# The last mixture of experts of a vision tower: every expert on every token, or sorted rows in blocks of 256

## The chip, the cores and the metric

The kernel runs on one core of a Trainium2 chip, as one program. The metric is the time of one execution on the device in microseconds (us). Engines are named as the profile names them: PE is TensorE's matmul, PEld its weight load, DVE VectorE, ACT ScalarE, POOL GpSimd, and SP the sync engine, which here only issues DMAs.

## The reference

128 images become 65 tokens each (64 patches and a class token), so 8320 tokens of 128 numbers. Two attention layers and two mixtures of experts follow, each behind a layer norm and added to the running sum. Only the last mixture is touched by the change:

```python
def _L1_ffn_ref(x, gate_w, gate_b, w1, b1, w2, b2):   # E, K = 8 experts, 2 of them per token; H = 128
    logits = jnp.einsum('bsh,he->bse', x, gate_w) + gate_b
    topk_vals, topk_idx = jax.lax.top_k(logits, K)
    topk_weights = jax.nn.softmax(topk_vals, axis=-1)
    mask = jax.nn.one_hot(topk_idx, E, dtype=topk_weights.dtype)
    weights = jnp.einsum('bske,bsk->bse', mask, topk_weights)
    h = jax.nn.relu(jnp.einsum('bsh,ehf->bsef', x, w1) + b1)          # f = 256
    expert_out = jnp.einsum('bsef,efh->bseh', h, w2) + b2
    return jnp.einsum('bseh,bse->bsh', expert_out, weights)
...
    h = h + _L1_ffn_ref(_layernorm(h, axis=-1), ...)
```

The weights of six of the eight experts are zero for each token. All arithmetic here is float32.

## The kernel before

The program is a chain of stages, each a block of its own with barriers between them: patch embedding, layer norm, attention, layer norm, the first mixture (`routed_mlp`), layer norm, attention, layer norm, and the last mixture, `dense_mixture`. `h` (the running sum) and `xn` (its layer norm) stay in SBUF all the time as 128 partitions by 8320 tokens.

`dense_mixture` goes over 65 tiles of 128 tokens in a loop with two buffers (`pipelined`, two tiles written out per turn). For a tile POOL copies its columns of `xn` and `h`. PE computes the logits (L1370). DVE finds the two best and makes the weights (L1450 to L1471), with an exponential on ACT (L1414). PE applies all eight experts: `up` gives 16 products of 128x128x128 into two PSUM banks (L1348), which ACT reads with bias and relu into `hidden_m` (L1405). `down` gives 16 more (L1360). PE also turns the weights (L1377), adds the old sum and the second bias through two matmuls (L1385, L1387), which ACT copies into `acc_m` (L1428). DVE then adds expert by expert, each times its weight (L1484, eight instructions per tile), and SP stores the tile (L1320). PE's order in one turn is: logits and `up` of this tile, mixed with weights, `down` and base of the tile before.

Waits are on counting semaphores: `hid_ps` and `hid_sb` between PE and ACT, `acc_done` between DVE and PE.

## Time and profile before

| what | value |
|---|---|
| median of 3 runs | 2122.07 us (2121.67 to 2122.54) |
| the profiled execution's own time | 2128.26 us |
| its span, first to last instruction | 2126.5 us |
| PE busy over the span | 1999.7 us, 94% |
| DVE, ACT, POOL busy | 1147.3, 1035.9, 629.5 us |
| last mixture, in the trace | from 1578.6 us to the end |

Durations come from the profiled execution, which took 6.2 us longer than the median. Busy times of PE are those of pipelined instructions, so they say that the engine had work, not that it ran at its peak. A float32 product of 128x128x128 stands in the trace as two matmul records and two weight loads. DMA-issuing instructions do not count as busy on any engine.

### The profile page before, as it was taken

To read this page: it belongs to the slowest core of one execution; us is meant where nothing else is said; L and a number is where in the kernel's file an instruction comes from. 1 tells how busy PE (TensorE), PEld (TensorE's weight loads), DVE (VectorE), ACT (ScalarE), POOL (GpSimd) and SP (SyncE) were. 2 spreads that over 40 slices of the span, in tenths; PEclk is the share of its full clock that TensorE was granted. 3 is DMA by queue.
4 is the path that set the end of the run, shared out by engine and by line. 5 is a ranking of instruction groups with operands and counts; after the bars stand their busy time and mean duration, and the time that the engine had idled before them with its cause. 6 is when DMAs were issued, how large, how long until landed. Compare 5 with 4: busy or idle time off the path is not lost. (4 is left out here: it accounts for less than half of the span.)

```text
span 2126.5 us, 69078 instructions
## 1 busy us (share of the span) xinstructions
PE 1999.7 (94%) x27049; PEld 1538.0 (72%) x27049; DVE 1147.3 (54%) x3517; ACT 1035.9 (49%) x3106; POOL 629.5 (30%) x866
## 2 busy tenths in 40 slices
PE   8999978999999898799989999999889999999999
PEld 3444446766776666387747888888659999999999
DVE  0000057877777777466654555555455555555555
ACT  0000055655655554444455555555366555565555
POOL 0000007777777777001102433333300000000000
PEclk9999989999999999869999999999889999999999
DMA  9878400000000000200000000000000000000000
GB/s 380 309 302 319 191 1 3 4 3 3 3 3 3 3 3 3 89 1 1 1 1 2 3 2 2 2 2 2 2 1 10 7 7 9 7 9 7 7 9 9
DMA packets 30122, 91.84 MB, mean 43 GB/s; under 512 B 5972, under 2 KB 15324, under 8 KB 29660
## 3 DMA queue, kind: packets, MB, share of 16 engines
q1 hardware_dynamic: 28238, 87.25, 10.8%
q8 instruction: 180, 2.95, 0.6%
q10 hardware_dynamic: 1678, 1.43, 0.2%
q14 instruction: 26, 0.21, 0.0%
HBM read 84.41 MB, written 4.26 MB: 42 GB/s over the span
## 5 line engine op out<-in xcount | busy, mean ns | idle before, releaser
L1405 ACT ACTIVATE hidden_m<-ps,s_f_b 128x128 f32<-128x128 f32 x1040 | 296.3, 368 | 224.3 <-PE ps L1348 220.8
L830 PE MATMUL ps<-xn,s_a_wqkv 128*128 128x260 f32 x1024 | 289.2, 406 | 13.5 <-ACT qk_a L576 8.3
L1348 PE MATMUL ps<-xn,s_f_w 128*128 (+1 forms) x2080 | 287.5, 282 | 0.4 <-ACT hidden_m L1405 0.4
L1484 DVE SCALAR_TENSOR_TENSOR acc_m<-ps,weights_m,acc_m 128x128 f32<-128x128 f32 x520 | 182.4, 351 | 153.9 <-ACT acc_m L1428 105.0
L1348 PEld LDWEIGHTS ps<-xn,s_f_w 128*128 128x128 f32 x2080 | 255.1, 193 | 8.4 <-ACT hidden_m L1405 0.7
L168 PE MATMUL ps<-x_chunk,s_w_tok 128*128 128x512 f32 x576 | 251.9, 599 | 6.3 <-DMA x_chunk<-in_x_main 6.3
L1360 PE MATMUL ps<-s_f_w,hidden_m 128*128 128x128 f32 x2080 | 253.6, 275 | 0.0
L1360 PEld LDWEIGHTS ps<-s_f_w,hidden_m 128*128 128x128 f32 x2080 | 242.6, 192 | 1.6
L830 PEld LDWEIGHTS ps<-xn,s_a_wqkv 128*128 128x128 f32 x1024 | 176.3, 192 | 57.0 <-ACT qk_a L576 20.4
L168 PEld LDWEIGHTS ps<-x_chunk,s_w_tok 128*128 128x128 f32 x576 | 109.8, 192 | 147.1 <-issue 147.1
L1334 POOL COPY xn_tile_m<-xn 128x128 f32 (+1 forms) x65 | 19.1, 293 | 535.3 <-PE ps L1387 494.2
L649 ACT ACTIVATE e_a<-e_a 128x585 f32<-128x585 f32 (+1 forms) x128 | 85.2, 665 | 182.2 <-DVE e_a L741 93.7
L588 ACT ACTIVATE resT_a<-ps 128x260 f32<-128x260 f32 x256 | 84.6, 383 | 147.8 <-PE ps L847 120.6
L195 DVE SCALAR_TENSOR_TENSOR h<-ps,s_b_tok,s_pos 128x512 f32 (+1 forms) x16 | 11.3, 747 | 249.1 <-PE ps L176 249.1
L912 PE MATMUL ps<-s_a_wqkv,xn_pair_a 128*64 128x256 f32 x1024 | 139.0, 391 | 2.4 <-issue 1.0
L729 DVE TENSOR_REDUCE neg_max_a<-ps 128x8 f32<-128x520 f32 x128 | 89.4, 699 | 93.8 <-PE ps L808 93.7
L548 POOL TENSOR_TENSOR prob_a<-e_a,inv_sum_a 128x512 f32<-128x512 f32 x64 | 66.7, 1042 | 247.0 <-DVE inv_sum_a L772 179.8
L1510 ACT ACT_TABLE_LOAD x1 | 1.3, 1283 | 268.1 <-PEq L101 268.1
L870 PE MATMUL ps<-horner_a,probT_a 64*64 64x64 f32 x2048 | 109.2, 219 | 7.5 <-issue 7.3
L880 PE MATMUL ps<-probT_a,horner_a 64*64 64x65 f32 x2048 | 108.8, 223 | 1.5 <-DVE horner_a L688 1.5
L870 PE MATMUL ps<-dv_a,probT_a 64*64 64x64 f32 x2048 | 105.7, 218 | 4.5 <-ACT dv_a L625 3.1
L532 POOL TENSOR_TENSOR kept_a<-e_a,keep_a 128x585 f32<-128x585 f32 x64 | 87.2, 1362 | 75.9 <-issue 63.6
(197 smaller groups left out, 4074.2 us busy)
## 6 DMA issues: line engine op xcount, KB each, us to landing
x_chunk<-in_x_main SPq DMA_DIRECT2D x96, 768.0 KB, 8.5
out<-acc_m SPq DMA_DIRECT2D x65, 64.0 KB, 1.5
s_f_w<-in_f_w SPq DMA_DIRECT2D x2, 1024.0 KB
x_ends<-in_x_tail SPq DMA_DIRECT2D x16, 96.0 KB, 10.7
s_w_tok<-in_w_tok SPq DMA_DIRECT2D x6, 192.0 KB, 7.5
s_a_wqkv<-in_a_wqkv ACTq DMA_DIRECT2D x1, 768.0 KB
s_a_wqkv<-in_a_wqkv SPq DMA_DIRECT2D x1, 768.0 KB
s_f_w<-in_f_w SPq DMA_DIRECT2D x2, 256.0 KB
```

The costliest lines, as they stand in the source:

```text
L168: last = nc.tensor.matmul(ps[:, bank, :], w_tok[:, k, :], xb[:, s, k, :], start=(k == 0), stop=False)
L532: nc.gpsimd.tensor_tensor(columns(kept, t.even), columns(e_of(t), t.even), columns(keep, t.even), ALU.mult).then_inc(kept_done, 1)
L649: nc.scalar.activation(columns(e_of(t), t.even), columns(e_of(t), t.even), ACT.Exp, scale=-SCALE)\
L729: last = nc.vector.tensor_reduce(neg_max[:, :, 0:CH], score(), AX.X, ALU.min)
L830: nc.tensor.matmul(ps[:, QK_BANK[i], 0:QUAD], w_qkv[:, c * P:(c + 1) * P], xn[:, t.h * QUAD:(t.h + 1) * QUAD], start=True, stop=True).then ...
L870: last = nc.tensor.matmul(ps[rows, 2 + n, col:col + DH], pt[rows, k, c, i, 1:SEQ], values[rows, i, c, :], start=True, stop=True)
L880: last = nc.tensor.matmul(ps[other, R_BANK[i], c * SEQ:c * SEQ + cols], values[rows, (t.j - 6) % 2, i, c, :], pt[rows, k, c, i, 0:cols], s ...
L912: last = nc.tensor.matmul(ps[b * DH:(b + 1) * DH, V_BANK, i * CH * DH:(i + 1) * CH * DH] .rearrange("p (c d) -> p c d", c=CH), xs[:, k, i ...
L1348: last = nc.tensor.matmul(ps[:, b % 2, i * P:i * P + n], w1[:, c * P:(c + 1) * P], xn[:, bass.ds(a.index * n, n)], start=True, stop=True)
L1360: last = nc.tensor.matmul(ps[0:n, 2 + b, (e % 4) * D:(e % 4 + 1) * D], hid[:, a.slot, c, :], w2[:, c, :], start=(f == 0), stop=(f == F1 // ...
L1405: last = nc.scalar.activation(hid[:, a.slot, c, :], ps[:, b % 2, i * P:i * P + n], ACT.Relu, bias=b1[:, c:c + 1])
L1484: nc.vector.scalar_tensor_tensor(out=acc[0:n, sl, :], in0=ps[0:n, 2 + e // 4, (e % 4) * D:(e % 4 + 1) * D], scalar=wt[0:n, sl, e:e + 1], i ...
```

## The change

`dense_mixture` is replaced by `sparse_mixture`, which applies only the two chosen experts. It has three parts.

**Routing and sorting.** Tokens are taken in 5 groups of 13 tiles; a tile is every 65th token, so partition p of tile t is token 65p + t (`tile_of`). For a group PE makes logits, turns `xn` into rows of tokens, and counts with `before` and `all_ones` how many earlier tokens chose each expert (`ranks`). DVE turns that into a row number per token and choice. POOL then writes, for each tile and each of the two choices, 128 rows of 130 numbers (the token's vector, its name and its weight) to those rows of a buffer in memory, `regions[k]`, with one indirect DMA: 130 in all. The region of an expert holds 34 x 256 rows. SP writes filler rows behind each expert's last row. PE and ACT also make `base` (old sum and bias), which now stays in SBUF. A table of blocks (row and expert of each) is worked out on DVE.

**Blocks.** For each choice there are 40 blocks of 256 rows, so 80, whether they hold tokens or only filler. For a block SP reads its row number from the table and loads 256 rows. PE turns them (2 products), DVE copies the result out. PE does `up` (2 products of 256 columns), ACT one relu and DVE the other, PE does `down` (4 products), and DVE multiplies by each row's weight. ACT copies the weights of the block's expert, 514 columns, into one of four buffers, after reading the column from the table. POOL writes the result with two indirect DMAs of 128 rows to `acc[k]` in memory, at the tokens' own rows: 160 in all. These blocks are written out, not looped, with four buffers, `up` one block behind `turn_block`, and `down` two behind. The buffer of rows is free again when the copy `own` is done.

**Sum.** `acc[0]` is loaded into `xn`'s place during the second choice, on SP's queue between two block loads; `acc[1]` is loaded into `h`'s place after the last scatter has landed. Each is 13 DMAs. DVE adds both to `base`, 13 + 13 instructions, and SP stores 13 pieces.

Outside of the stage only the loading of this mixture's weights differs, into one tensor `f1_all` per expert.

```diff
+ROW = D + 2
+BLOCK_ROWS = 256
 
...
+def sparse_mixture(nc, tokens, h, xn, ps, ident, before, all_ones, gate_w, gate_b, expert_ids, w_all, b2,
+                   regions, acc, out):
...
+            for k in range(K):
+                def step(j, at, k=k):
+                    a = at(0)
+                    if a:
+                        g = a.index + k * NB
+                        row = sp.value_load(entry(row_i, k, a.index), min_val=0,
+                                            max_val=REGION * E1 + BLOCK_ROWS * (E1 - 1))
+                        freed(sp, own_done, g, R)
+                        sp.dma_start(blk[:, a.slot], regions[k][bass.ds(row, BLOCK_ROWS), :]
+                                     .rearrange("(h p) c -> p h c", p=P)).then_inc(loaded[a.slot], 16)
+                        if k == 1 and isinstance(a.index, int) and a.index == 2 * R - 1:
+                            for i in range(R):
+                                sp.wait_ge(added[i], 32 * NB // R)
+                            for c in range(PIECES):
+                                sp.dma_start(over_tiles(xn, c), in_memory(acc[0], c)).then_inc(piece_in[c], 16)
+                straight(sp, NB, R, 0, 2 * R, step)
+            for i in range(R):
+                sp.wait_ge(added[i], K * 32 * NB // R)
+            for c in range(PIECES):
+                sp.dma_start(over_tiles(h, c), in_memory(acc[1], c)).then_inc(last_in[c], 16)
+            for c in range(PIECES):
+                sp.wait_ge(finished, c + 1)
+                sp.dma_start(in_memory(out, c), base[:, c * PT:(c + 1) * PT, :]).then_inc(stored, 16)
+            sp.wait_ge(stored, 16 * PIECES)
...
+            for g in range(G):
+                pool.wait_ge(slot_done, g + 1)
+                for s, (t0, t1) in enumerate(SUBS):
+                    pool.wait_ge(xt_sb, S * g + s + 1)
+                    for t in range(t0, t1):
+                        for k in range(K):
+                            nc.gpsimd.indirect_dma_start(
+                                regions[k][:, :],
+                                bass.IndirectOffsetOnAxis(ap=slot_i[:, g % 2, t, k:k + 1], axis=0),
+                                rows[:, g % 2, t, 2 * k:2 * k + ROW], None).then_inc(sent[g % 2], 16)
+            for g in range(K * NB):
+                for half in range(2):
+                    pool.wait_ge(y_done, 2 * g + half + 1)
+                    nc.gpsimd.indirect_dma_start(
+                        acc[g // NB][:, :], bass.IndirectOffsetOnAxis(ap=goal[:, g % R, half:half + 1], axis=0),
+                        ys[:, g % R, half, :], None).then_inc(added[g % R], 16)
...
+            def logits(g):
+                for t in range(T):
+                    last = nc.tensor.matmul(logits_ps()[:, t, :], tile_of(xn, g * T + t), gate_w[:, :],
+                                            start=True, stop=True)
+                last.then_inc(l_ps, 1)
+
+                                                   tile_of(xn, g * T + t), ident[:, :])
+                    last.then_inc(xt_ps, 1)
...
+                nc.tensor.matmul(rank_at(), before[:, :], chosen[:, g % 2], start=True, stop=False)
+                for i in range(T):
+                    last = nc.tensor.matmul(rank_at()[:, i + 1:T + 1], all_ones[:, :],
+                                            chosen[:, g % 2, i:i + 1].to_broadcast([P, T - i, K, E1]),
+                                            start=False, stop=(i == T - 1))
...
+            logits(0)
+            turn_x(0)
+            ranks(0)
+            for g in range(G):
+                if g + 1 < G:
+                    logits(g + 1)
+                    turn_x(g + 1)
+                    ranks(g + 1)
+                turn_weights(g, 0)
+                for s in range(S):
+                    if s + 1 < S:
+                        turn_weights(g, s + 1)
+                    bases(g, s)
...
+            def turn_block(g, slot, k):
+                filled(pe, loaded[slot], g, slot, 16)
+                freed(pe, bt_sb, g, 2)
+                for half in range(2):
+                    last = nc.tensor.transpose(turned(slot)[:, half * P:(half + 1) * P], blk[:, slot, half, X_AT[k]],
+                                               ident[:, :])
...
+                for f in range(2):
+                    nc.tensor.matmul(ps[:, 1 + 2 * (slot % 2) + f, 0:BLOCK_ROWS], wb[:, slot, f * P:(f + 1) * P],
+                                     xt[:, slot % 2, :], start=True, stop=True).then_inc(up_ps, 1)
...
+                for half in range(2):
+                    for f in range(2):
+                        last = nc.tensor.matmul(ps[:, 5 + slot % 2, half * D:(half + 1) * D],
+                                                hid[:, slot % 2, f, half * P:(half + 1) * P],
+                                                wb[:, slot, F1 + f * P:F1 + (f + 1) * P],
+                                                start=(f == 0), stop=(f == 1))
...
+                    a = at(1)
+                    if a:
+                        up(a.index + k * NB, a.slot)
+                    a = at(0)
+                    if a:
+                        turn_block(a.index + k * NB, a.slot, k)
+                    a = at(2)
+                    if a:
+                        down(a.index + k * NB, a.slot)
...
+            def fetch_weights(g, slot, column):
+                freed(act, y_ps, g, R)
+                nc.scalar.activation(wb[:, slot, :], w_all[:, :, :].rearrange("p e c -> p (e c)")[
+                    :, bass.ds(column, WB)], ACT.Copy).then_inc(w_sb, 1)
...
+                    a = at(2)
+                    if a:
+                        act.wait_ge(w_sb, a.index + k * NB + 1)
+                        relu(a.index + k * NB, a.slot)
+                    a = at(0)
+                    if a:
+                        column = act.value_load(entry(col_i, k, a.index), min_val=0, max_val=WB * (E1 - 1))
+                        fetch_weights(a.index + k * NB, a.slot, column)
+                straight(act, NB, R, 2, R, step)
...
+            for g in range(G):
+                choose(g)
+                seat(g)
...
+            def copy_xt(g, slot, k):
+                dve.wait_ge(bt_ps, g + 1)
+                freed(dve, up_ps, g, 2, 2)
+                nc.vector.tensor_copy(xt[:, slot % 2, :], ps[:, 7 * (slot % 2), 0:BLOCK_ROWS]).then_inc(bt_sb, 1)
+                freed(dve, y_done, g, R, 2)
+                nc.vector.tensor_copy(own[:, slot], blk[:, slot, :, OWN_AT[k]]).then_inc(own_done, 1)
...
+            def relu(g, slot):
+                dve.wait_ge(up_ps, g * 2 + 2)
+                freed(dve, y_ps, g, 2)
+                nc.vector.tensor_scalar(hid[:, slot % 2, 1, :], ps[:, 2 + 2 * (slot % 2), 0:BLOCK_ROWS],
+                                        wb[:, slot, 2 * F1 + 1:2 * F1 + 2], 0.0, ALU.add, ALU.max).then_inc(hid1, 1)
...
+            def weigh(g, slot, k):
+                dve.wait_ge(own_done, g + 1)
+                emptied(dve, added[slot], g, slot, 32)
+                nc.vector.tensor_copy(goal[:, slot], own[:, slot, :, NAME[k]])
+                dve.wait_ge(y_ps, g + 1)
+                for half in range(2):
+                    nc.vector.tensor_scalar(ys[:, slot, half, :], ps[:, 5 + slot % 2, half * D:(half + 1) * D],
+                                            own[:, slot, half, WEIGHT[k]:WEIGHT[k] + 1], None,
+                                            ALU.mult).then_inc(y_done, 1)
...
+            for c in range(PIECES):
+                dve.wait_ge(piece_in[c], 16)
+                nc.vector.tensor_tensor(base[:, c * PT:(c + 1) * PT, :], base[:, c * PT:(c + 1) * PT, :],
+                                        over_tiles(xn, c), ALU.add).then_inc(summed, 1)
+            for c in range(PIECES):
+                dve.wait_ge(summed, c + 1)
+                dve.wait_ge(last_in[c], 16)
+                nc.vector.tensor_tensor(base[:, c * PT:(c + 1) * PT, :], base[:, c * PT:(c + 1) * PT, :],
+                                        over_tiles(h, c), ALU.add).then_inc(finished, 1)
...
-        dense_mixture(nc, tokens, h, xn, ps, S["ident"], S["f1_gate"], S["f1_gate_b"], S["expert_ids"],
-                      S["f1_w1"], S["f1_b1"], S["f1_w2"], S["f1_b2"], out)
+        sparse_mixture(nc, tokens, h, xn, ps, S["ident"], S["before"], S["all_ones"], S["f1_gate"], S["f1_gate_b"],
+                       S["expert_ids"], S["f1_all"], S["f1_b2"], regions, acc, out)
```

The next rows are PE's instructions, in the middle of the last mixture, before: one tile's turn of the loop (`s_f_w` in L1348 is the first weight, in L1360 the second; register instructions stand between).

```order
L1370 MATMUL ps<-s_f_gate,xn_tile_m 128x8
L1348 MATMUL ps<-xn,s_f_w 128x128 x4
L1377 MATMUL ps<-s_ident,weights_m 8x128
L1360 MATMUL ps<-s_f_w,hidden_m 128x128 x8
L1348 MATMUL ps<-xn,s_f_w 128x128 x4
L1385 MATMUL ps<-s_ident,h_tile_m 128x128
L1387 MATMUL ps<-s_f_b,weightsT_m 128x128
```

After these come 4, 8 and 4 more of L1348, L1360 and L1348. In the changed kernel the same place on PE, one step of the blocks (line numbers are the changed kernel's: L1545 turns rows, L1555 is `up`, L1564 is `down`):

```order
L1555 MATMUL ps<-pad_rows_m,rows_m 128x256 x2
L1545 MATMUL ps<-s_ident,rows_m 128x128 x2
L1564 MATMUL ps<-rows_m,pad_rows_m 128x128 x4
```

So 37 products a tile, 65 times, become 8 products a block, 80 times, and `up` now has 256 columns. On POOL, the end of its program was two copies a tile:

```order
L1334 COPY xn_tile_m<-xn 128x128
L1335 COPY h_tile_m<-h 128x128
```

Now POOL's part of the stage reads (L1463 the scatters into `regions`, L1470 those into `acc`):

```order
L1452 MEMSET pad_rows_m 128x4224
L1455 IOTA pad_rows_m 128x32 x2
L1463 DMA expert_rows<-rows_m,slot_i_m 71680x130 x130
L1470 DMA out_rows<-pad_rows_m,block_goal_m 12416x128 x160
```

All 290 indirect DMAs stand in one row on POOL's one queue, and it does nothing else. On ACT one step of the blocks is this (L1652 reads the column, L1635 copies the weights, L1641 is the relu):

```order
L1652 TENSOR_LOAD block_column_m
L1652 ISA x2
L1635 ISA
L1635 ACTIVATE rows_m<-s_f_all 128x514
L1641 ACTIVATE pad_rows_m<-ps,rows_m 128x256
```

Where ACT had 16 relus of 128 columns a tile, it has now two instructions a block and a read into a register ahead of them.

## Rows read from the trace of the kernel before

**Rows 1.** The page: span, then busy time of each engine.
```profile
span 2126.5 us, 69078 instructions
PE 1999.7 (94%) x27049; PEld 1538.0 (72%) x27049; DVE 1147.3 (54%) x3517; ACT 1035.9 (49%) x3106; POOL 629.5 (30%) x866
```
**Rows 2.** Busy time by stretch: the mixture, inside it, and the patch embedding's loads.
```profile
core 0: us, PE busy (x) PEld busy (x) DVE busy (x) ACT busy (x) POOL busy (x), PEclk, DMA share, GB/s
1578.60:2126.50 547.90, 543.48 (x4615) 525.82 (x4615) 305.19 (x1365) 322.48 (x1236) 34.29 (x130) 0.99 0.03 8
1600.00:1700.00 100.00, 100.00 (x857) 96.83 (x856) 56.28 (x252) 59.42 (x229) 6.44 (x25) 1.00 0.03 8
60.00:160.00 100.00, 100.00 (x238) 43.29 (x237) 4.23 (x6) 0.00 (x0) 0.00 (x0) 1.00 0.82 318
```
**Rows 3.** Waits in the mixture: who waited for whom, us, times, longest.
```profile
POOL xn_tile_m L1334 <- PE ps L1387: 494.2, 63, 11.7
ACT hidden_m L1405 <- PE ps L1348: 220.8, 194, 8.5
```
**Rows 4.** The chain that ended last, mixture: shares, then one piece.
```profile
by line: PE ps L1348 45.7%; PE ps L1360 42.3%; PE ps L1387 4.9%; PE ps L1385 2.6%; PE ps L1370 1.5%; PE ps L1377 1.3%; ACT hidden_m L1405 0.4%; DVE acc_m L1484 0.3%; ACT L1414 0.2%; issue 0.1%; POOL xn_tile_m L1334 0.1%; POOL h_tile_m L1335
...
1612.73 1.79 PE ps L1360 x16
```
**Rows 5.** Groups by line, PE: busy us, mean ns of one.
```profile
L168 PE MATMUL ps<-x_chunk,s_w_tok 128*128 128x512 f32 x576 | 251.9, 599 | 6.3 <-DMA x_chunk<-in_x_main 6.3
L1370 PEld LDWEIGHTS ps<-s_f_gate,xn_tile_m 128*128 128x128 f32 x130 | 19.9, 194 | 2.6 <-POOL h_tile_m L1335 2.6
```
**Rows 6.** Groups by line, DVE and ACT.
```profile
L704 DVE COPY probT_a<-ps 128x512 f32<-128x512 f32 x64 | 44.3, 692 | 101.5 <-PE ps L945 101.5
L723 DVE TENSOR_TENSOR h<-ps,h 128x256 f32 x26 | 11.1, 425 | 0.0
L741 DVE TENSOR_SCALAR e_a<-ps,neg_max_a 128x65 f32<-128x65 f32 x64 | 17.7, 277 | 0.0
L1459 DVE CAST index_m<-index_m 128x2 f32<-128x2 uint32 x65 | 11.0, 169 | 2.3
L1454 DVE MAX8 top_m<-logit_m 128x8 f32<-128x8 f32 x65 | 10.7, 165 | 2.8
L613 ACT ACTIVATE v_raw_a<-ps 128x512 f32<-128x512 f32 x64 | 38.2, 597 | 29.1 <-PE ps L912 28.7 <-POOL v_alpha_a L536 0.4
L588 ACT ACTIVATE resT_a<-ps 128x260 f32<-128x260 f32 x256 | 84.6, 383 | 147.8 <-PE ps L847 120.6 <-PE ps L880 27.0
```
**Rows 7.** Groups by line, POOL.
```profile
L1334 POOL COPY xn_tile_m<-xn 128x128 f32 x60 | 17.6, 293 | 467.0 <-PE ps L1387 467.0
L548 POOL TENSOR_TENSOR prob_a<-e_a,inv_sum_a 128x512 f32<-128x512 f32 x64 | 66.7, 1042 | 247.0 <-DVE inv_sum_a L772 179.8 <-issue 67.1
L478 POOL MEMSET cls_queries_a<- 128x1040 f32 x2 | 1.9, 965 | 345.9 <-POOLq L219 345.9
```
**Rows 8.** The output tile's stores: issue in ns (min/median/max), and us to landing.
```profile
L1320 SPq DMA_DIRECT2D out<-acc_m x65: 332/332/353, 1595.6 to 2124.6; - x65
...
DMA to landing us min/median/max: 1.5/1.5/2.7
```
**Rows 9.** Windows between stages and in the first mixture.
```profile
1520.00:1530.00 10.00, 7.34 (x147) 5.89 (x151) 5.45 (x10) 3.44 (x11) 5.08 (x8) 1.00 0.01 2
1530.00:1550.00 20.00, 12.17 (x72) 8.13 (x69) 1.12 (x3) 6.16 (x11) 1.11 (x2) 0.57 0.00 1
900.00:940.00 40.00, 35.48 (x154) 32.13 (x155) 22.59 (x103) 14.88 (x32) 0.00 (x0) 0.50 0.00 1
```

More of the change, by code:

```diff
@@ L36 @@
 EPS = 1e-5
+REGION = 34 * 256
 BANK = 512
 CHUNK_IMAGES = 8
+ROW = D + 2
+BLOCK_ROWS = 256
 class At:
@@ new lines, in sparse_mixture @@
+        pad_i = sb("pad_place_m", [P, K, E1], I32)
+        base = sb("base_m", [P, TILES, D])
+        limit = sb("limits_m", [P, K, E1, LB])
+        over = sb("over_limit_m", [P, K, E1, LB])
+        blocks = sb("blocks_of_m", [P, K, E1])
+        upto = sb("not_after_m", [P, E1, E1])
+        part = sb("prefix_terms_m", [P, K, E1, E1])
+        end = sb("end_block_m", [P, K, E1])
+        number = sb("block_number_m", [P, NB])
+        past = sb("past_m", [P, K, NB, E1])
+        gone = sb("gone_m", [P, K, NB, E1])
@@ new lines, in _ @@
+            nc.gpsimd.iota(number[:, :], [[1, NB]], base=0, channel_multiplier=0,
+                           allow_small_or_imprecise_dtypes=True).then_inc(consts, 1)
+            nc.gpsimd.memset(pad[:, :, :, :], 0.0).then_inc(pads_made, 1)
+            pool.wait_ge(pads_made, 1)
+            for column in (1, D + 2):
+                nc.gpsimd.iota(pad[:, :, :, column], [[BLOCK_ROWS, 2 * E1], [P, 2]], base=tokens,
+                               channel_multiplier=1, allow_small_or_imprecise_dtypes=True).then_inc(pads_made, 1)
@@ L1488, in _, with chained, settle, ids @@
-            pipelined(dve, tokens // n, SL, D_, SL, step)
+            done = [0]
+            def chained(ins):
+                done[0] += 1
+                ins.then_inc(chain, 1)
+            def settle():
+                dve.wait_ge(chain, done[0])
+            def ids(shape, axes):
+                t = expert_ids[:, 0:E1]
+                for a in axes:
+                    t = t.unsqueeze(a)
+                return t.to_broadcast(shape)
+            nc.vector.memset(chosen[:, :, T], 0.0)
@@ new lines, in _ @@
+            settle()
+            for k in range(K):
+                last = nc.vector.tensor_tensor(part[:, k], blocks[:, k, :].unsqueeze(1).to_broadcast([P, E1, E1]),
+                                               upto[:, :, :], ALU.mult)
+            chained(last)
+            settle()
+            chained(nc.vector.tensor_reduce(end[:, :, :], part[:, :, :, :], AX.X, ALU.add))
+            settle()
+            for k in range(K):
+                last = nc.vector.tensor_tensor(past[:, k], number[:, :].unsqueeze(2).to_broadcast([P, NB, E1]),
+                                               end[:, k, :].unsqueeze(1).to_broadcast([P, NB, E1]), ALU.is_ge)
@@ new lines, in _ @@
+            chained(last)
+            settle()
+            for k in range(K):
+                last = nc.vector.tensor_tensor(gone[:, k], past[:, k], blocks[:, k, :].unsqueeze(1)
+                                               .to_broadcast([P, NB, E1]), ALU.mult)
+            chained(last)
+            chained(nc.vector.tensor_reduce(expert[:, :, :], past[:, :, :, :], AX.X, ALU.add))
+            settle()
+            chained(nc.vector.tensor_reduce(first[:, :, :], gone[:, :, :, :], AX.X, ALU.add))
@@ new lines, in _ @@
+            settle()
+            chained(nc.vector.tensor_scalar(base_row[:, :, :], expert[:, :, :], float(REGION), None, ALU.mult))
+            for k in range(K):
+                last = nc.vector.tensor_tensor(row_f[:, k, :], number[:, :], first[:, k, :], ALU.subtract)
+            chained(last)
+            settle()
+            chained(nc.vector.scalar_tensor_tensor(out=first[:, :, :], in0=row_f[:, :, :], scalar=float(BLOCK_ROWS),
+                                                   in1=base_row[:, :, :], op0=ALU.mult, op1=ALU.add))
@@ L1605, in vit_tower @@
         h = ctx.enter_context(nc.sbuf_tensor("h", [P, tokens], FP32))
+        assert tokens + BLOCK_ROWS <= REGION and REGION % BLOCK_ROWS == 0
+        regions = [nc.dram_tensor(f"expert_rows{k}", (E1 * REGION + E1 * BLOCK_ROWS, ROW), FP32, kind="Internal").ap()
+                   for k in range(2)]
+        acc = [nc.dram_tensor(f"out_rows{k}", (tokens + 2 * E1 * BLOCK_ROWS, D), FP32, kind="Internal").ap()
+               for k in range(2)]
         xn = ctx.enter_context(nc.sbuf_tensor("xn", [P, tokens], FP32))
```

495 lines of the change are left out of this document (304 added, 191 removed).

## The prediction

> **What bounds the kernel now.** I read the busy times first. PE is at 94% of the span, no other engine above 54% [rows 1]. A share over the whole span says little about one stage, so I cut the trace: the last mixture runs from 1578.60 us to the end, 547.9 us, and PE is busy for 543.5 of them, at a granted clock of 0.99 [rows 2]. The waits agree: POOL and ACT wait for PE (494 and 221 us) and no long wait of PE for anyone stands there [rows 3]. The chain that ended last is PE for 98% of this stretch [rows 4]. So the stage is worth what its matmuls cost.
>
> What one costs comes from the stretch of 100 us in which PE never stops: 857 matmul records [rows 2]. A tile has 71 records (65 tiles; 64 for `up` and `down`, 7 for the rest), so 857/71 = 12.07 tiles, 8.28 us each. A piece of the chain has 16 records of `down` in 1.79 us, 0.112 us a record, or 0.224 us for a float32 product of 128 columns [rows 4]. 64 records are 7.17 us of the 8.28. The other 1.11 us are four products (logits, turned weights, two for the base), 0.28 us each. With 512 columns a record takes 251.9/576 = 0.437 us [rows 5]; between the two, 256 columns take about 0.22 us a record, 0.44 us a product.
>
> The profiled execution took 2128.26 us, the median is 2122.07. I work out the stage's new length, and apply the difference to the median.
>
> **What the change takes away.** The whole stage, 547.9 us. What stands outside of it keeps its instructions, except for loads of weights that fall early and are hidden in both.
>
> **What it adds, part by part.** The unknown that decides is c, the time that one indirect DMA of 128 rows holds POOL's queue. There are 130 + 160 of them, in order, on one engine. No row of the trace shows one. From below, SP needs 0.332 us to issue a plain DMA of 128 rows [rows 8], where hardware makes the addresses. From above, if POOL were held until the data lands, it would be issue and landing, 0.33 + 1.5 = 1.83 us [rows 8]. In between, POOL's instruction on 512 elements takes 1.04 us, its copy of 128 columns 0.29 us [rows 7]. An indirect DMA makes an address for each of 128 rows in software, one by one, which is nearer to POOL's long instruction than to its copy. I take c = 1.3 us, between 1.04 and 1.83, and keep 0.33 and 1.83 as ends.
>
> The Trainium skill, DMA: Bandwidth & Descriptors, section on the anatomy of a DMA from GpSimd, gives about 2.0 us plus the bytes over 436e3 per DMA, mostly the receipt at its end. An estimate by that page, if the whole term held the queue for 64 KB, is 2.15 us; the sum below would then be 708 us instead of 461. The page itself puts most of it behind the issue, where it can overlap, and no row here tells which.
>
> 1. *Start, 16 us.* The first scatter needs logits, chosen experts, ranks and row numbers of group 0. PE: 13 logits and 13 turned tiles at 0.28 to 0.56 us (the upper end at half clock, since the granted clock was 0.57 between the last attention and its layer norm [rows 9]), some 9 us, then 14 small rank products, 2 us. DVE runs 26 instructions of the MAX8 kind, 0.165 us each or less when they follow one another [rows 6], and about ten more: 7 us, partly beside PE. Row numbers: five instructions of up to 208 elements, 2 us. POOL's memset of 4224 columns costs 4224/1040 x 0.965 = 3.9 us [rows 7] and is hidden in this.
>
> 2. *Scatters of tokens, 130 x 1.3 = 169 us.* Beside them PE has, per group of 13 tiles, 65 products at 0.28 and the ranks: 18.2 + 2 = 20 us, against 26 x 1.3 = 34 us on POOL. DVE has about 9 us, ACT less. They are hidden while c is over 0.78 us; without that cover the part costs 100 us. Another price that the trace does not show is the weight load from every 65th column: 39 products a group read so. A load of 128 neighbouring columns takes 0.19 us [rows 5]; if such a one took twice that, two to a product, PE's group grows by 39 x 2 x 0.19 = 15 to 35 us, level with POOL: still nothing. SBUF — State Buffer in the Trainium skill, its remark on cachelines, says that each access to a new 16-byte line pays a penalty, which speaks for that price; no row here reads so.
>
> 3. *Handover, 10 us.* The last scatter lands (1.5 us [rows 8]), SP reads a row number and loads 133 KB (2 to 3 us), and a first block goes through turn, copy, `up`, relu, `down` and the multiply, about 4 us, before POOL has work again. The table of blocks is made while POOL still scatters group 4.
>
> 4. *Blocks, 80 x 2.8 = 224 us.* POOL: 2 x 1.3 = 2.6 us a block. PE: two turns 0.45, `up` 2 x 0.44 = 0.88, `down` 4 x 0.224 = 0.90, so 2.23 us. DVE: two instructions of 256 columns at 0.425, two of 128 at about 0.3, two tiny ones at 0.17 [rows 6], 1.8 us. ACT: a copy of 514 columns 0.60 and a relu of 256 at 0.38 [rows 6], 0.98 us, and a register read that the trace does not show: between nothing and a landing, 1.5 us [rows 8], so at most 2.5 us. DMA: the output tile's 128 rows are a share of 0.03 of 16 engines [rows 2], 0.03 x 16 x 8.28/128 = 0.03 us a row; 512 rows a block over 16 engines are 1.0 us. POOL sets the pace with four engines close behind it, so I add 0.2 us for steps in which one of them is late.
>
> 5. *Loading the first sum, 6 us.* SP puts 13 DMAs, 4.26 MB, between two block loads on its queue. At 318 GB/s [rows 2] that is 13.4 us, and the next block load lands about 16 us later. Four buffers cover 4 x 2.8 = 11 us. The rest is a stall of the blocks, with the drain between the two choices about 6 us in all.
>
> 6. *End, 36 us.* After the last product POOL scatters twice, 2.6 us, and 1.5 us pass until they land. Then 4.26 MB come in and 4.26 MB go out, 8.52 MB/318 GB/s = 26.8 us, and two landings and the issue of the first piece, 4 us. DVE adds 26 pieces of 640 columns, at (692/512) x 640 = 0.86 us each [rows 6] 22 us, half before the loads are in. Sum 35, taken as 36.
>
> 16 + 169 + 10 + 224 + 6 + 36 = 461 us, against 547.9: 87 us less. The median would be 2122.07 - 87 = **2035 us**. As a function of c the stage is 84 + 290c, where 84 = 16 + 10 + 6 + 36 + 80 x 0.2; it equals 547.9 at c = 1.60 us. At c = 1.15 to 1.5 it is 417 to 519, the result 1991 to 2093.
>
> **The rivals.**
>
> *Cheap scatters.* If a scatter costs as POOL's 512-element instruction does, 1.04 us, the tokens take 135 us, and a block 2.5 us, paced by PE and ACT: 16 + 135 + 10 + 200 + 6 + 36 = 403, result 1977. For it: the work of an indirect DMA on POOL moves no data. Against: it makes two times 128 addresses. At c = 0.33 PE paces both parts: 16 + 100 + 10 + 184 + 6 + 36 = 352, result 1926.
>
> *Slower: a scatter holds POOL.* At c = 1.83, where it waits for its own landing, the stage is 84 + 531 = 615, result 2189. It decides from c = 1.60 on. For it: every row moves by its own address and one engine makes them all, and the changed program has nothing to put beside them but a wait. Against: on SP's queue the next issue does not wait for the landing before it.
>
> *The clock.* Where the work on PE gets thin its granted clock falls to half: 0.57 between the last attention and layer norm with 12 of 20 us busy, but also 0.50 in the first mixture with 35 of 40 us busy; with 7.3 of 10 us busy in the last attention it was 1.00 [rows 9]. Blocks that leave PE idle for 0.6 us in 2.8 may fall on either side. At 1.2 GHz a block costs PE 2 x 2.23 = 4.46 us, 357 instead of 224, and the groups 40 us instead of 34, 30 more in all: 461 + 133 + 30 = 624, result 2198. With only the blocks slow for half of the time it is 461 + 66 = 527, result 2101. Against the full fall: at half speed PE would be busy all the time, and in long stretches of full work it had its full clock.
>
> **How the numbers follow.** Chances: my forecast (c from 1.1 to 1.6) 0.50; cheap scatters 0.15; a scatter that holds POOL 0.23; the clock, or a chain between engines as slow as it, 0.12. The likeliest case alone reaches from 1991 to 2093. The range that holds 8 in 10 goes from 1950, below the cheap case, to 2185, nearly to the held one. What a measurement of this kernel can tell is about 0.2%, 4 us. Faster: 0.48 of the first, all of the second, a third of the last: 0.67. Within 0.2%: 0.03. Slower: 0.30.
>
> **What would show it.** In the changed profile: the scatters into `regions` follow each other at a steady distance, which is c, and the sum of the first part is 130 times that (step 2). Blocks: 2.8 us from one load of SP to the next, and DVE waiting for `added`, the landed scatters, more than for PE (step 4). If DVE instead waits for PE and PEclk reads 0.5, it is the clock. A gap of some 6 us in PE at the eighth block of the second choice is step 5. From the last block to the end about 36 us with high GB/s (step 6). The prediction is wrong if c is outside of 1.1 to 1.6, or if a step of the blocks is over 3.3 us while POOL is idle.

## The result and the profile after

The changed kernel takes **2000.96 us** (median of 4 runs, 1999.92 to 2006.15) against 2122.31 us of the kernel before, run beside it (2121.67 to 2124.63): a ratio of 0.9431, 95% interval 0.9413 to 0.9449, 121 us less. The forecast was 2035, with a range of 1950 to 2185. The profiled execution took 2000.72 us.

The page, span and busy times, against [rows 1]:

```profile
span 1998.7 us, 60392 instructions
PE 1753.3 (88%) x24144; PEld 1274.2 (64%) x24144; DVE 1020.6 (51%) x2949; ACT 835.0 (42%) x2096; POOL 881.3 (44%) x1033
```

POOL has gained 252 us of work and PE lost 246; a reader of this row alone would still call PE the bound. The stage shows otherwise. It now runs from 1571.10 us to the end, 427.6 us instead of 547.9, and the windows of busy time cut it as the prediction did, into start, scatters of tokens, handover, blocks and end; the last window is a steady piece of the blocks (compare [rows 2]):

```profile
1571.10:1584.70 13.60, 12.66 (x62) 11.82 (x62) 6.56 (x56) 3.33 (x6) 5.37 (x7) 0.50 0.61 126
1584.70:1749.40 164.70, 110.70 (x530) 97.90 (x529) 32.21 (x235) 28.52 (x60) 125.10 (x130) 0.58 0.22 68
1749.40:1762.70 13.30, 7.97 (x25) 6.14 (x26) 2.96 (x11) 3.48 (x6) 0.00 (x0) 0.50 0.30 75
1762.70:1972.50 209.80, 169.91 (x1097) 149.41 (x1095) 126.56 (x482) 85.05 (x154) 154.94 (x160) 0.93 0.40 118
1972.50:1998.70 26.20, 0.00 (x0) 0.00 (x0) 10.53 (x13) 0.00 (x0) 0.00 (x0) 0.50 0.88 328
...
1800.00:1850.00 50.00, 43.82 (x278) 37.79 (x278) 29.05 (x119) 21.23 (x39) 37.81 (x41) 1.00 0.37 105
```

In a steady 50 us of the blocks PE is busy for 43.8 us and POOL for only 37.8, and yet POOL is the bound. Its groups by line say why: behind "idle before" almost all of the time stands under "issue", that is, nobody kept it waiting.

```profile
L1470 POOL DMA_INDIRECT out_rows<-pad_rows_m,block_goal_m x160 | 154.9, 968 | 68.2 <-issue 43.3 <-DVE pad_rows_m L1800 24.9
L1463 POOL DMA_INDIRECT expert_rows<-rows_m,slot_i_m x130 | 125.1, 962 | 47.5 <-issue 39.3 <-DVE slot_i_m L1734 8.2
```

A scatter is 0.96 us busy and 0.30 us of gap that belongs to it: **c = 1.263 us** from start to start, the mean of the 91 scatters of the blocks between 1762.71 and 1877.67 us; in the first part it is 164.7/130 = 1.267. The waits between 1578 and 2000 us (who waited for whom, us, times, longest; compare [rows 3], where POOL waited 494 us for PE):

```profile
POOL out_rows L1470 <- issue: 43.3, 142, 0.3
DVE block_goal_m L1797 <- DMA out_rows<-pad_rows_m,block_goal_m: 56.1, 54, 2.0
POOL out_rows L1470 <- DVE pad_rows_m L1800: 24.9, 18, 13.6
```

DVE waits 54 times for a scatter's landing. POOL waits for DVE's products for 24.9 us in all, and 19.8 of these are two gaps: the handover (13.6, of which 0.3 belongs to c) and one gap of 6.2 us in the second choice, the stall of step 5 in the prediction (the timeline of POOL):

```profile
1877.67 0.96 POOL L1470 DMA_INDIRECT out_rows<-pad_rows_m,block_goal_m  x1 [0.30 <-issue]
1884.81 0.96 POOL L1470 DMA_INDIRECT out_rows<-pad_rows_m,block_goal_m  x1 [6.18 <-DVE pad_rows_m L1800]
1886.07 0.96 POOL L1470 DMA_INDIRECT out_rows<-pad_rows_m,block_goal_m  x1 [0.30 <-issue]
```

On SP's queue the cause stands ahead of it: the 13 loads of the first sum take 8.6 us to issue, 0.3 to 1.0 us each, and the block load behind them lands 8.3 us after its own issue instead of about 2 (first the SP timeline, then the chain that ended last):

```profile
1864.85 7.80 SPq L1431 DMA_DIRECT2D xn<-out_rows  x13
1873.41 21.64 SPq L1425 DMA_DIRECT2D rows_m<-expert_rows  x10
...
1873.41 8.29 DMA rows_m<-expert_rows
1881.75 0.69 PE ps L1545 x2
1882.44 1.71 PE ps L1564 x8
```

The load that comes late is the ninth of the second choice, but POOL's gap lies ahead of the seventh block's scatters. PE does its products in the program's order, and the program has the turn of a block ahead of the `down` of the block two before it. So PE stands at the ninth block's turn for 8.5 us, while the seventh block's `down`, which needs nothing of that load, waits behind it.

### The profile page after: what moved, and what is told of

Its sections match the earlier page's. It is cut to its first block and busy times, and to the rows that moved or that the text cites. A ratio compares the mean times of both kernels' runs of the same rounds, so it can differ in the third digit from the quotient of the medians.

```text
span 1998.7 us, 60392 instructions
## 1 busy us (share of the span) xinstructions
PE 1753.3 (88%) x24144; PEld 1274.2 (64%) x24144; DVE 1020.6 (51%) x2949; ACT 835.0 (42%) x2096; POOL 881.3 (44%) x1033
## 3 DMA queue, kind: packets, MB, share of 16 engines
q8 instruction: 191, 3.13, 0.6%
## 5 line engine op out<-in xcount | busy, mean ns | idle before, releaser
L1470 POOL DMA_INDIRECT out_rows<-pad_rows_m,block_goal_m x160 | 154.9, 968 | 68.2 <-issue 43.3
L1463 POOL DMA_INDIRECT expert_rows<-rows_m,slot_i_m x130 | 125.1, 962 | 47.5 <-issue 39.3
L1555 PE MATMUL ps<-pad_rows_m,rows_m 128*128 128x256 f32 x320 | 90.8, 408 | 18.1 <-issue 15.8
L1261 POOL TENSOR_TENSOR h<-h,mlp_gated 128x320 f32<-128x320 f32 x26 | 22.4, 863 | 187.9 <-DVE mlp_gated L1241 187.9
L579 ACT ACTIVATE qk_a<-ps 128x260 f32<-128x260 f32 x256 | 92.2, 388 | 28.6 <-PE ps L833 25.3
L883 PE MATMUL ps<-probT_a,cls_values_a 64*64 64x1 f32 x2048 | 91.8, 187 | 6.0 <-issue 5.7
```

What stands on the lines that cost most here:

```text
L579: nc.scalar.activation(qk[:, t.j // 2, c, :], ps[:, QK_BANK[i], 0:QUAD], ACT.Identity if bias is not None else ACT.Copy, bias=bias[:, i:i ...
L883: last = nc.tensor.matmul(ps[other, R_BANK[i], c * SEQ:c * SEQ + cols], values[rows, (t.j - 6) % 2, i, c, :], pt[rows, k, c, i, 0:cols], s ...
L1463: nc.gpsimd.indirect_dma_start(regions[k][:, :], bass.IndirectOffsetOnAxis(ap=slot_i[:, g % 2, t, k:k + 1], axis=0), rows[:, g % 2, t, 2 * ...
L1470: nc.gpsimd.indirect_dma_start(acc[g // NB][:, :], bass.IndirectOffsetOnAxis(ap=goal[:, g % R, half:half + 1], axis=0), ys[:, g % R, half, ...
L1555: nc.tensor.matmul(ps[:, 1 + 2 * (slot % 2) + f, 0:BLOCK_ROWS], wb[:, slot, f * P:(f + 1) * P], xt[:, slot % 2, :], start=True, stop=True) ...
```

## The experiments

Twelve runs. Apart from the totals I give the stage by itself, from its first logits product (1571.1 us in the changed kernel) to the end. That product starts anywhere between 1570.0 and 1576.3 us in these traces, although the code ahead of it is the same, so a total carries noise of up to 6 us that the stage doesn't.

| run | time, us (runs) | ratio to before, 95% interval | stage, us | against 427.6 |
|---|---|---|---|---|
| extra_128 | 2096.35 (2) | 0.9869 (0.9842 to 0.9897) | 523.3 | +95.7 |
| extra_64 | 2095.11 (2) | 0.9864 (0.9837 to 0.9891) | 517.7 | +90.1 |
| extra_thin | 2095.85 (2) | 0.9867 (0.9840 to 0.9894) | 523.0 | +95.4 |
| half_down | 2001.82 (4) | 0.9424 (0.9403 to 0.9445) | 427.0 | -0.6 |
| load_spread | 1994.95 (5) | 0.9395 (0.9383 to 0.9408) | 422.3 | -5.3 |
| blocks_early | 1993.30 (5) | 0.9385 (0.9372 to 0.9397) | 417.0 | -10.6 |
| early_spread | 1983.31 (5) | 0.9346 (0.9333 to 0.9359) | 407.8 | -19.8 |
| bases_first | 2004.99 (5) | 0.9445 (0.9430 to 0.9459) | 427.5 | -0.1 |
| extra_8 | 2216.34 (2) | 1.0430 (1.0399 to 1.0460) | disturbed | |
| extra_plain | 2111.90 (3) | 0.9938 (0.9916 to 0.9961) | disturbed | |
| down_twice | 2124.14 (8) | 0.9997 (0.9972 to 1.0021) | disturbed | |
| down_twice_again | 2031.89 (4) | 0.9566 (0.9550 to 0.9582) | 455.8 | +28.2 |

My theory: POOL's queue sets the pace at c for each indirect DMA, and all else is hidden up to 2 x c = 2.53 us a block. The first rival: PE, or a chain through it, sets the pace, since it is the busier engine.

**Does POOL pace, and what is c made of?** A third indirect DMA in each block:

```diff
+                nc.gpsimd.indirect_dma_start(
+                    scratch[:, :], bass.IndirectOffsetOnAxis(ap=goal[0:128, g % R, 0:1], axis=0),
+                    ys[0:128, g % R, 0, 0:128], None).then_inc(added[g % R], 16)
```

extra_64 has `goal[0:64 ...]` and `ys[0:64 ...]`, extra_thin `ys[..., 0:16]`. In all of them a block's buffers count as free only when the third DMA has landed too (48 instead of 32 on `added`).

> Every block of the second part gets a third indirect DMA on POOL, of 128 rows of 128 numbers into a tensor that nobody reads: 80 more in all, nothing is left out, and the block's buffers come free only when it has landed too. Theory (POOL's queue sets the pace of the blocks, 1.263 us for each indirect DMA): 80 x 1.263 = 101 us more than the changed kernel's 2001, less up to 6 us because four buffers then cover more of the stall at the first sum's load: 2096 to 2102, and the distance between scatters stays 1.26. Rival (PE or a chain of engines sets the pace and POOL has room of its own): less than 60 us more. A third case: with 3.8 us a block PE is busy for about half of the time only; if its granted clock falls to 0.5 a block costs PE 4.0 to 4.4 us, 2115 to 2150, and POOL shows idle time that PE ends.

> As extra_128, but the third indirect DMA of a block writes 64 rows of 128 numbers instead of 128 rows. It asks what the 1.26 us of a scatter are made of. If they are paid for each row (an address made for each in software, as I argued before the result), the extra one costs 0.63 us and the kernel takes 80 x 0.63 = 50 us more than 2001, 2051; its busy time on POOL reads 0.48 us. If they are paid for each instruction, it costs as much as extra_128, 2102. In between (0.3 us of issue and the rest by rows): 0.78 us each, 2063.

> As extra_128, but the third indirect DMA of a block writes 128 rows of only 16 numbers (64 bytes instead of 512). If POOL's 1.26 us are paid for making addresses or for each instruction, it costs as much as extra_128: 2096 to 2102. If they are paid for moving the bytes (the queue takes no more until the data has been drained), the extra one costs about an eighth of that and the issue, 0.3 to 0.45 us, and the kernel takes 2025 to 2037.

extra_128 came out as the theory of the pace said: 80 x 1.263 = 101.0, less 5.9 for the gap at the first sum's load (6.18 less the 0.30 of any scatter), which is gone, is 95.1; the stage grew by 95.7. The distance stayed 1.26. The other two settle what c is. The groups by line of extra_128, extra_64 and extra_thin, in this order:

```profile
L1474 POOL DMA_INDIRECT scratch_rows<-pad_rows_m,block_goal_m x80 | 77.4, 967 | 24.4 <-issue 24.4
```
```profile
L1474 POOL DMA_INDIRECT scratch_rows<-pad_rows_m,block_goal_m x80 | 72.6, 908 | 24.4 <-issue 24.4
```
```profile
L1474 POOL DMA_INDIRECT scratch_rows<-pad_rows_m,block_goal_m x80 | 77.4, 967 | 24.4 <-issue 24.4
```

An eighth of the bytes costs the same, and half of the rows saves 0.06 us of 0.96. So c is paid for each instruction, hardly for rows, not for bytes. The guess that c is made of rows gave 2051 us for extra_64, 44 us too little.

> As extra_64, but the third indirect DMA of a block writes only 8 rows. POOL's busy time was 0.96 us for 128 rows and 0.905 us for 64, a slope of 0.85 ns a row. If this line goes on, 8 rows take 0.86 us busy and 1.16 us with the issue, and the kernel takes 80 x 1.16 = 93 us more than the changed kernel's 2001, less the 6 to 7 us that the other extras showed: 2086 to 2089. If the price for few rows is a small one (a step per row or per 64 rows), it takes 2025 to 2045.

> As extra_128, but the third DMA of a block is a plain one on POOL's queue, 128 rows of 128 numbers to neighbouring rows of the unread tensor, with no indices. If the 1.26 us belong to any DMA that POOL's software prepares, it costs the same, 2094 to 2098. If they belong to the indirect form, the plain one holds POOL for about as long as SP's 0.33 us or less, and the kernel takes at most 80 x 0.4 = 32 us more than 2001: 2001 to 2033.

extra_plain's third DMA is `nc.gpsimd.dma_start(scratch[g * P:(g + 1) * P, :], ys[:, g % R, 0, :])`. Both totals missed: in these two and in down_twice engines stood still in the scatters of tokens (below). What the extra DMA costs can still be read where POOL has its work in time. The timeline of extra_8, then that of extra_plain:

```profile
1873.43 0.88 POOL L1474 DMA_INDIRECT scratch_rows<-pad_rows_m,block_goal_m  x1 [0.30 <-issue]
1874.62 1.00 POOL L1471 DMA_INDIRECT out_rows<-pad_rows_m,block_goal_m  x1 [0.30 <-issue]
```
```profile
1871.31 0.96 POOL L1471 DMA_INDIRECT out_rows<-pad_rows_m,block_goal_m  x1 [0.30 <-issue]
1872.28 0.58 POOL L1474 DMA_DIRECT2D scratch_rows<-pad_rows_m  x1
1873.15 0.98 POOL L1471 DMA_INDIRECT out_rows<-pad_rows_m,block_goal_m  x1 [0.30 <-issue]
```

Eight rows hold POOL for 0.88 us and the gap, 1.18 us, against 1.16 expected. A plain DMA holds it for 0.58 us and has no gap ahead of it; a block takes 3.13 us instead of 2.53, so it costs 0.60 us, half of an indirect one and nearly twice SP's 0.332 us [rows 8].

**Is PE hidden, and by how much?** half_down takes two of the four products of `down` away, so that its output lacks half of the second layer's sum; down_twice does all four twice, with the same output. Of half_down's edit (the first two lines; `start` and `stop` follow it) and down_twice's (the last two):

```diff
-                    for f in range(2):
+                    for f in range(1):
...
-                for half in range(2):
+                for half in (0, 1, 0, 1):
```

> PE leaves out the second half of the hidden layer in down: 2 products of 128 columns a block instead of 4, so the output holds half of the second layer's sum. Nothing else changes. Theory (POOL paces the blocks at 2.53 us, and PE, which does a step in 1.98 us when work is queued for it, waits): no change, 1998 to 2003. Rival (PE, or a chain through it, paces the blocks): 80 x 0.45 = 36 us less, 1965; one third of that, 1989, if PE paces only the blocks in which it runs slow or catches up. A fall of the granted clock with the thinner work would make it slower, by up to 80 x 0.6 = 50 us.

> PE does the 4 products of down twice in each block, 0.9 us more work at full clock; the output is the same. A step of PE that has its work queued took 1.98 us in the changed kernel, so it takes 2.88 us here, more than POOL's 2.53. Theory (PE is hidden up to 2.53 us and sets the pace above that): 80 x 0.35 = 28 us more than 2001, less what of the two stalls is caught up, 2025 to 2032, and POOL now waits for DVE's rows in most blocks. Rival (PE and POOL take turns instead of overlapping, so that each us on PE is a us on the blocks): 80 x 0.9 = 72 us more, 2073. If PE's own step were longer than I read (2.4 us), 62 us more.

> The same program as down_twice, run again, since in the three kernels that ran together (extra_8, extra_plain, down_twice) PE and ACT stood still for some 90 us in the scatters of tokens, whose code those kernels don't change. If that belongs to the chip or the moment of that call, the scatters of tokens now follow each other without a gap (164 us from first to last, not 240), and the kernel takes what the theory of PE's pace says: 2025 to 2032 if PE's step is 2.88 us, 2073 if every us of PE counts. If it belongs to the program (where its code lies), the gaps are there again at the same places and the time is 2115 to 2130.

half_down changed nothing (stage -0.6 us), though PE was then busy for 34.8 instead of 43.8 us in the window 1800 to 1850: 9 us less work in 50, not one of them on the path. The rival falls. down_twice_again took 28.2 us more, as expected from 80 x (2.88 - 2.53), and its waits from 1765 to 2020 us have turned round: POOL waits 78 times, DVE for PE instead of for landings.

```profile
POOL out_rows L1470 <- DVE pad_rows_m L1800: 71.7, 78, 14.8
DVE pad_rows_m L1800 <- PE ps L1564: 66.7, 80, 2.3
```

Its timeline of PE gives one step, 1833.94 to 1836.81, 2.87 us without a gap:

```profile
1833.94 1.03 PE L1555 MATMUL ps<-pad_rows_m,rows_m 128*128 128x256 f32 x4
1834.81 0.38 PE L1545 MATMUL ps<-s_ident,rows_m 128*128 128x128 f32 x2
1835.03 1.95 PE L1564 MATMUL ps<-rows_m,pad_rows_m 128*128 128x128 f32 x16
1836.81 1.03 PE L1555 MATMUL ps<-pad_rows_m,rows_m 128*128 128x256 f32 x4
```

Of these, 0.89 us are the second `down` (what one took in the changed kernel's chain at full clock). So PE needs 2.87 - 0.89 = 1.98 us a block in the changed kernel, and 0.55 us of slack lie in each 2.53.

The first run of this program took 2124 us, 92 more. What was different comes under "The stand-still".

**Can the two gaps be taken out?** load_spread puts one load of the first sum behind every second block load:

```diff
-                            for c in range(PIECES):
+                        if k == 1 and isinstance(a.index, int) and 2 * R - 1 <= a.index < 2 * R - 1 + 2 * PIECES \
+                                and (a.index - 2 * R + 1) % 2 == 0:
+                            c = (a.index - 2 * R + 1) // 2
```

blocks_early lets the first choice's blocks start while the second choice's last 13 scatters still run:

```diff
+                for ks in ((0, 1),) if g + 1 < G else ((0,), (1,)):
...
+                                    .then_inc(sent[g % 2] if g + 1 < G or k == 0 else late, 16)
...
+                if k:
+                    sp.wait_ge(late, 16 * T)
```

> The 13 loads of the first sum go to SP's queue one at a time, each behind every second block load, instead of all 13 ahead of one block load; nothing is left out. Theory: the block load that today queues behind 4.26 MB comes 8.5 us late for PE and leaves POOL idle for 6.2 us once; spread, no block load is later than 2 us and the four buffers cover that. 6 us less than the changed kernel's 2001: 1994 to 1997, and no gap of over 1 us in POOL's row of scatters in the second choice. Rival (the stall is paid back by blocks that follow faster, or each small load costs a little of its own): no change, 1999 to 2003.

> In the last group of tokens POOL writes the 13 tiles' rows of the first choice first, then the 13 of the second; SP loads the first choice's blocks as soon as the first choice's rows have landed and only the second choice's blocks wait for the rest. The rings of block rows and weights move to places that are free by then. Nothing is left out. Theory: the handover of 13.3 us, in which POOL has no work, comes to lie beside 13 x 1.263 = 16.4 us of scatters: about 12 to 13 us less, 1988 to 1990, with no gap of POOL over 1.5 us between the two rows of scatters. Rival (the filler rows, the table of blocks or the first PE steps at half clock are late too, so that the blocks can't start so early): a gain of 5 us or less, 1996 to 2001.

> The edits of load_spread and blocks_early together. Theory: two stalls in different places of one row of 290 scatters, so the gains add: 18 to 20 us less than the changed kernel's 2001, 1981 to 1983, and 6.5% less than the kernel before (ratio 0.934). If one gap only makes room for another (PE late after the earlier start, say), less than 14 us.

load_spread came out as expected: 5.3 us in the stage, and the gap is gone. blocks_early fell short: 10.6 us in the stage instead of 12 to 13, and a total of 1993.30 us instead of 1988 to 1990. The handover vanished, with 1.26 us from the last scatter of tokens to the first of a block (its timeline of POOL):

```profile
1753.47 0.96 POOL L1467 DMA_INDIRECT expert_rows<-rows_m,slot_i_m  x1 [0.31 <-issue]
1754.73 0.96 POOL L1475 DMA_INDIRECT out_rows<-pad_rows_m,block_goal_m  x1 [0.30 <-issue]
```

but the second gap grew from 6.2 to 7.3 us, and beside it stood two of 0.7 and 1.35 us. With both edits the gains more than add, 19.8 us in the stage against 18 to 20 expected (the second gap goes at its larger size), and POOL's waits in the stage of early_spread leave nothing to take away:

```profile
POOL out_rows L1477 <- issue: 40.2, 132, 0.3
POOL expert_rows L1469 <- issue: 39.3, 129, 0.3
POOL out_rows L1477 <- DVE pad_rows_m L1806: 8.5, 28, 0.3
```

No wait of POOL is over 0.3 us there but the first, for row numbers: from the first scatter to the end of the last it is 367.9 us, and 290 x 1.263 = 366.3. At 1983.31 us (ratio 0.9346) this version beats both kernels; it is faster than the changed one by 17.7 us in the totals, and the two intervals are apart.

**Does the order of ranks and base rows matter?** bases_first moves `logits(g + 1)`, `turn_x(g + 1)` and `ranks(g + 1)` on PE, and `exponential` and `copy_x` on ACT, behind the base rows of group g.

> Undoes one part of the change, the ranks ahead of base rows: PE and ACT do a group's base rows first and the logits, turned rows and ranks of the next group behind them. Nothing is left out. Theory: POOL's 26 scatters of a group take 33 us and PE's work for a group 20 to 28 us, so the order inside of a group is hidden: 2001, or up to 4 us more at the second group. Rival (the order matters: DVE's chain from ranks to row numbers then ends behind POOL's last scatter of the group before): 3 to 8 us more at each of four groups, 2013 to 2033, seen as POOL waiting for DVE's row numbers.

The stage is 427.5 us against 427.6, and POOL waits only once for row numbers, at the start, 8.2 us as before. So this part of the change is worth nothing here. The total is 4.0 us higher; in the profiled execution the stage starts 4.2 us later, and nothing was edited ahead of it.

**The stand-still.** extra_8, extra_plain and down_twice ran on the same chip. In all three the scatters of tokens, which none of them edits, took some 50 us longer, and POOL waited for row numbers of a later group three times, 28.0, 11.4 and 11.5 us; the handover was 27 to 29 us. In extra_8 and down_twice the later steps of the blocks were uneven as well; in extra_plain only one gap stood there, 2.7 us. ACT's timeline in down_twice, where the changed kernel has gaps of 2 to 3 us at these lines:

```profile
1596.24 1.13 ACT L1596 ACTIVATE rows_m<-ps 128x384 f32<-128x384 f32 x2 [0.63 <-issue]
1618.41 0.59 ACT L1605 ACTIVATE weightsT_m<-ps 8x512 f32<-8x512 f32 x1 [21.03 <-remote]
1625.42 0.48 ACT L1605 ACTIVATE weightsT_m<-ps 8x384 f32<-8x384 f32 x1 [6.42 <-remote]
1661.81 0.60 ACT L1613 ACTIVATE base_m<-ps 128x512 f32<-128x512 f32 x1 [35.91 <-remote]
```

"remote" is a wait for which the trace has no releaser. The same program on another chip had none of this and took 2031.89 us, so the program alone doesn't bring it about; whether the chip or the moment did can't be told. extra_8 and extra_64, one number apart, say the same. The kernel before ran beside them at its usual 2123.47 us. PE was fully at work again only when POOL had run out of scatters at about 1654 us: busy for 19.2 us of 1670 to 1690, after 0.7 of 1630 to 1650. One guess is that code was fetched late while POOL's DMAs ran, since this stage is written out straight. The trace's DMA records of the instruction queues don't bear it out. In down_twice_again packets of 16 KB start at 1591.7, 1609.2 and 1638.9 us; in down_twice one starts at 1591.0 and the next only at 1665.8, but ACT and PE are at work again at 1661.8 and 1662.5, ahead of it. The missing packets may be a consequence of the stand-still as well as its cause, and the cause stays open.

## Why the prediction was right

The decision was right for its reason: one queue, 290 indirect DMAs in a row, at c = 1.263 us against 1.3 assumed and a break-even of 1.60. The size was less good: the stage was 33 us shorter than the sum, so the change saved 121 us where 87 were forecast. The five windows above against the sum:

| step | forecast | measured | off by |
|---|---|---|---|
| 1 start | 16 | 13.6 | -2.4 |
| 2 scatters of tokens | 169 | 164.7 | -4.3 |
| 3 handover | 10 | 13.3 | +3.3 |
| 4, 5 blocks and first sum's load | 224 + 6 | 209.8 | -20.2 |
| 6 end | 36 | 26.2 | -9.8 |
| sum | 461 | 427.6 | -33.4 |

- *Step 1.* PE was busy for 12.7 of 13.6 us at a granted clock of 0.50, as the dearer price assumed.
- *Step 2.* Hidden as forecast: PE was busy for 110.7 of 164.7 us at a granted clock of 0.58. The load of every 65th column is settled by the weight loads' groups by line. First from 1596 to 1598 us (granted clock 1.00), where L1516 reads every 65th column and L1520 neighbours, then from 1753 to 1762 us (0.50), where L1555 reads neighbours:

```profile
L1516 PEld LDWEIGHTS ps<-s_ident,h 128*128 128x128 f32 x7 | 1.7, 327 | 0.0
L1520 PEld LDWEIGHTS ps<-s_f_b,weightsT_m 8*128 8x128 f32 x4 | 0.5, 185 | 0.1
```
```profile
L1555 PEld LDWEIGHTS ps<-pad_rows_m,rows_m 128*128 128x128 f32 x10 | 2.9, 325 | 2.3 <-issue 1.0 <-ACT rows_m L1635 1.0
```

L1520 loads only 8 rows, but the blocks' loads of neighbours with 128 rows take as long, 0.189 us for L1555 from 1800 to 1850 us at 1.00. So at full clock the stride makes it 0.327 us instead of 0.19, 1.7 times as much and not 2; at half clock a load of neighbours takes 0.325 us as well, and L1516 took 0.325 us on average over the whole of this part, so there the stride costs nothing. The Trainium skill, SBUF — State Buffer, remark on cachelines, says that an access to a new 16-byte line pays a penalty; the trace agrees at full clock and shows no such penalty at half clock.
- *Step 3, short by 3.3.* The first steps of PE ran at half clock, and its program puts three blocks' turns and two `up` ahead of the first `down`. The chain that ended last (start, us, what):

```profile
1754.79 2.04 PE ps L1555 x4
1756.83 0.44 PE ps L1545 x2
...
1757.87 2.04 PE ps L1555 x4
...
1760.34 1.71 PE ps L1564 x8
```

`up` took 2.04 us where later blocks take 0.87. From the first turn, at 1753.52, to the end of that `down` it was 8.5 us, and I had about 4 for all of this.
- *Step 4, mis-sized.* "I add 0.2 us for steps in which one of them is late" was the largest error, 16 us. Almost no step was late: 75 of the 79 distances from block to block were 2.52 to 2.54 us, and the other four were the gap, the block behind it and the last two. The second is 0.037 x 160 = 6 us in c. PE's own price was too high as well, 2.23 against 1.98, because I priced a turn as two records and it has one (0.22 us for both halves); nothing hung on it. The rows had the count: a tile's seven other records are two each for logits and the two base products, and one for the turned weights. With 16 + 16 for `up` and `down` that also makes 36 products a tile, not 37.
- *Step 5.* 6.18 us against 6, and load_spread shows the cause by taking it away. The late load landed 16.9 us after the first of the 13 was issued, against about 16. The drain between the two choices, which the 6 us also held, made no gap on POOL. That the gap's size was met is in part luck, since the sum went by the four buffers alone and not by the `down` that stood behind the late turn on PE.
- *Step 6, over by 9.8.* 2.6 us were counted twice, since the last two scatters are part of the 80 blocks. 1 us was rounding (35 taken as 36). The rest is overlap: I put loads and stores of 4.26 MB each at 26.8 us, and 5.5 us of landings and issue on top, and all of it took 26.2 us, at 328 GB/s.

The argument for c was wrong, and that its value came near was luck. "An indirect DMA makes an address for each of 128 rows in software, one by one, which is nearer to POOL's long instruction than to its copy": extra_64 and extra_8 show that a row costs 0.7 to 0.9 ns, some 0.1 us of the 1.26 for all 128. Had the change moved 64 rows with each DMA, that reasoning would have given 0.65 us where 1.20 is true, and 290 DMAs would have been 160 us off.

The rivals. The held scatter (c = 1.83): no, a scatter lands 2.3 us after its issue and the next one starts after 1.26. The Trainium skill, DMA: Bandwidth & Descriptors, on the anatomy of a DMA from GpSimd, gave an estimate of 2.15 us. That is near the 2.3 us to the landing, and the trace agrees with the page that a part of this time can overlap, but it is 1.0 us of the 2.3 and not most of it: POOL is held for the other 1.26. The cheap scatter: no, at 1.04 the token part would have been 135 us. The clock: the granted clock was 0.58 on average in the first part, where that was hidden, and 1.00 in the steady blocks with 43.8 of 50 us busy, where at half speed PE would have set the pace. It stayed at 1.00 with 34.8 of 50 us busy too (half_down). It did fall inside of the blocks, to 0.57 from 1854 to 1862 us, where PE had stood still for 3.6 us at the change from the first choice to the second, and again around the 6.2 us gap. POOL had no gap at the first of these places.

## What to carry to other kernels

Price a row of indirect DMAs by their number, not by rows or bytes, and ask of every other engine only whether it stays below that pace. Here 9 us of PE's work in 50 could go, and nothing changed, while one added indirect DMA a block cost 1.2 to 1.26 us each. Then look for the places where the pacing queue is empty: a bulk load put whole between small urgent ones, and a wait for all rows where some would do, were 19.8 us together. A few lines took out the first, and some twenty, with buffers moved to other places, the second.

## What the runs showed of the hardware that I had not expected

- An indirect DMA holds POOL for 0.96 us with 128 rows, 0.91 with 64 and 0.88 with 8, and 0.30 us of gap with it. A plain one of 128 rows holds it for 0.58 us.
- The widths of rows don't show on POOL: 16 numbers a row cost as much as 128.
- On one chip ACT stood still for up to 36 us at a time and PE for up to 30 while POOL issued scatters, in three kernels, and not in the same program on another. A total that misses by 90 us is worth a look at stretches that the edit doesn't touch, before a theory is bent to it.
